# Down-projection of a six-layer attention and feed-forward kernel as nine reduced-precision products, with GpSimd splitting the gated values and the weights

## The reference

```python
def ffn_layer(x, g, bln, W1, b1, W2, b2):
    mu = x.mean(-1, keepdims=True)
    var = ((x - mu) ** 2).mean(-1, keepdims=True)
    xn = (x - mu) / jnp.sqrt(var + 1e-05) * g + bln
    hg = xn @ W1 + b1
    a, gate = jnp.split(hg, 2, -1)
    return a * jax.nn.gelu(gate, approximate=False) @ W2 + b2
for i in range(DEPTH):
    x = attn_layer(shift_tokens(x), Wqkv[i], q_scale[i], k_scale[i], Wo[i]) + x
    x = ffn_layer(shift_tokens(x), ln_g[i], ln_b[i], W1[i], b1[i], W2[i], b2[i]) + x
```

## Time and profile before

| | |
|---|---|
| median of 3 runs | 1655.81 us |
| the profiled execution | 1654.67 us, of which 1652.9 us are the span of the trace |
| TensorE (PE) busy | 95% of the span |
| VectorE (DVE), ScalarE (ACT), GpSimd (POOL) busy | 79%, 77%, 65% |
| one slot of the loop | 30.0 us |

### The profile page before, as it was taken

The page is one execution under the profiler, slowest core; times in us unless marked ns, Lnnn a source line. Parts: engine busy times, 40 slices in busy tenths (PEclk is TensorE's granted clock), DMA queues, the critical chain, the costliest instruction groups (busy, mean ns, idle before and its releaser), DMA issues.

```text
span 1652.9 us, 89828 instructions
## 1 busy us (share of the span) xinstructions
PE 1566.3 (95%) x36944; PEld 1275.7 (77%) x36944; DVE 1305.2 (79%) x1944; ACT 1280.4 (77%) x2012; POOL 1074.3 (65%) x788
## 2 busy tenths in 40 slices
PE   7898699999999999999999999999999999999986
PEld 3575578888888888888888888888888888888865
DVE  5575778788887887888878888888788888887853
ACT  5796557788887888878888788788787887887853
POOL 2203767768767769667678676777776787767631
PEclk9899799999999999999999999999999999999989
DMA  3000224223324232333222342322343323232221
GB/s 128 2 0 1 55 68 113 63 60 75 92 56 113 71 74 65 79 106 82 61 64 69 95 111 57 71 71 65 85 110 75 71 53 91 71 76 63 60 69 34
DMA packets 75728, 116.75 MB, mean 71 GB/s; under 512 B 17294, under 2 KB 27276, under 8 KB 74764
## 3 DMA queue, kind: packets, MB, share of 16 engines
q1 hardware_dynamic: 75660, 115.99, 28.2%
HBM read 19.04 MB, written 1.05 MB: 12 GB/s over the span
## 4 chain that ended last, share of the span: by engine, by line
PE 90%; issue 4%; DVE 3%; ACT 2%; DVEq 0%; POOL 0%; DMA 0%; ACTq 0%; SPq 0%; POOLq 0%
PE ps L646 14%; PE ps L912 10%; PE ps L887 10%; PE ps L838 9%; PE ps L763 9%; PE ps L766 8%; PE ps L767 8%; PE ps L979 4%; PE ps L831 3%; PE ps L928 3%; PE ps L930 2%; PE ps L929 2%; PE ps L635 1%; DVE h L1648 1%; PE ps L919 1%
## 5 line engine op out<-in xcount | busy, mean ns | idle before, releaser
L448 POOL TENSOR_TENSOR arena<-arena 128x1024 f32<-128x1024 f32 x192 | 456.5, 2378 | 74.6 <-DVE arena L1578 60.9
L457 POOL TENSOR_TENSOR arena<-arena,rnorm 128x1024 f32<-128x1024 f32 x192 | 361.7, 1905 | 208.4 <-ACT rnorm L1189 208.3
L646 PE MATMUL ps<-cst,arena 64*128 64x64 f32 x6656 | 290.1, 230 | 27.1 <-issue 6.0
L646 PEld LDWEIGHTS ps<-cst,arena 64*128 64x128 f32 x6656 | 249.1, 140 | 84.8 <-issue 71.3
L1178 ACT ACTIVATE arena<-ps 128x1024 f32<-128x1024 f32 x192 | 196.8, 1025 | 100.7 <-DVE arena L1578 99.6
L1574 DVE TENSOR_TENSOR arena<-ps,rope 128x1024 f32<-128x1024 f32 x192 | 233.8, 1218 | 26.5 <-PE ps L767 26.5
L1578 DVE TENSOR_TENSOR arena<-ps,rope 128x1024 f32<-128x1024 f32 x192 | 233.3, 1215 | 0.0
L766 PE MATMUL ps<-wqkv_lo,x_hi 128*128 128x512 f32 x576 | 228.8, 397 | 0.0
L767 PE MATMUL ps<-wqkv_hi,x_hi 128*128 128x512 f32 x576 | 228.2, 396 | 0.0
L1588 DVE TENSOR_REDUCE norm<-arena 128x16 f32<-128x1024 f32 x192 | 224.5, 1210 | 0.3 <-ACT arena L1178 0.2
L763 PE MATMUL ps<-wqkv_hi,x_lo 128*128 128x512 f32 x576 | 201.4, 431 | 0.6 <-issue 0.6
(11 more groups left out here) (137 smaller groups left out, 2733.7 us busy)
## 6 DMA issues: line engine op xcount, KB each, us to landing
v_sb<-v_nat SPq DMA_DIRECT2D x576, 130.0 KB
v_sb<-v_nat SPq DMA_DIRECT2D x192, 65.0 KB
wqkv_sb<-wqkv SPq DMA_DIRECT2D x6, 1536.0 KB, 6.3
v_sb<-v_sb SPq DMA_DIRECT2D x96, 65.0 KB
wo_sb<-wo SPq DMA_DIRECT2D x6, 512.0 KB, 3.7
w_sb<-w SPq DMA_DIRECT2D x6, 341.0 KB, 4.0
x<-xT SPq DMA_DIRECT2D x1, 1024.0 KB, 4.8
scl<-scales SPq DMA_DIRECT2D x6, 128.0 KB, 6.1
```

The costliest lines, as they stand in the source:

```text
L448: pool.tensor_tensor(t_cos[:, m, j, :], t_cos[:, m, j, :], t_sin[:, j, :], ALU.add)\
L457: pool.tensor_tensor(x, x, rnorm[:, H * j:H * j + H].unsqueeze(2).to_broadcast([P, H, D]), ALU.mult).then_inc(s[done], 1)
L646: mm = pe.transpose(ps[0:width, bank + t, 64 * c:64 * c + 64], src[r], ident[r, r], tile_position=(64 * t, 0))
```

## The change

`f_g` becomes a buffer of its own, and VectorE's product is written in place. GpSimd gets `part_gated` in each slot from 3 to 46: it copies the product, rounded, into `f_ah` and writes the rest into `f_al`. In slots 8L+3 it also gets `split_down`, which does the same with W2 (`w2_hi`, `w2_lo`). TensorE's `down` in the loop becomes `down_parted`, nine matmuls. The units 44 to 47, whose down-projections come behind the loop, keep `down` in float32; units 45 to 47 have a buffer each for the product (`f_last`). Gates now wait until the parts of the unit before are made (`f_parted`) and not for its product. Six buffers are cleared at the start, and two buffers of the first stage move into `arena`.

```diff
+            def part_gated(f):
+                pool.wait_ge(s["f_prod"], CREDIT + 3 * f + 3)
+                pool.wait_ge(s["f_down"], CREDIT + f)
+                pool.sem_inc(s["pool_waited"], 1)
+                pool.tensor_copy(f_ah[:, :, :], f_g[:, :, :]).then_inc(s["f_rounded"], 1)
+                pool.wait_ge(s["f_rounded"], CREDIT + f + 1)
+                pool.tensor_tensor(f_al[:, :, :], f_g[:, :, :], f_ah[:, :, :].bitcast(F32), ALU.subtract)\
+                    .then_inc(s["f_parted"], 1)
+
+            def split_down(layer):
+                pool.wait_ge(s["w_2_loaded"], 32 * layer + 32)
+                pool.wait_ge(s["f_down"], CREDIT + B * layer)
+                pool.sem_inc(s["pool_waited"], 1)
+                for i in (0, 2):
+                    rows, w = (P, slice(0, 2)) if i == 0 else (HT[2][1], slice(2, 3))
+                    pool.tensor_copy(w2_hi[0:rows, w, :], w2_sb[0:rows, w, :]).then_inc(s["w2_high"], 1)
+                    pool.wait_ge(s["w2_high"], CREDIT + 2 * layer + 1 + i // 2)
+                    part = pool.tensor_tensor(w2_lo[0:rows, w, :], w2_sb[0:rows, w, :],
+                                              w2_hi[0:rows, w, :].bitcast(F32), ALU.subtract)
+                part.then_inc(s["w2_ready"], B)
...
                     rotate(g + 1, 0, 0)
                     low(g + 1, 1)
                     rotate(g + 1, 0, 1)
+                    if ff:
+                        part_gated(g - LAG)
+                    if after == 3:
+                        split_down(layer)
                     if after == 7:
                         table(layer, 1)
                         split_weights(layer, 2)
...
+            def down_parted(f):
+
+                pe.wait_ge(s["f_parted"], CREDIT + f + 1)
+                pe.wait_ge(s["w2_ready"], CREDIT + f + 1)
+                out = ps[:, 1, 0:N]
+                for i in range(3):
+                    r = slice(0, HT[i][1])
+                    high = f_ah[r, i, :]
+                    pe.matmul(out, w2_lo[r, i, :], high, start=(i == 0), stop=False)
+                    pe.matmul(out, w2_hi[r, i, :], f_al[r, i, :], start=False, stop=False)
+                    mm = pe.matmul(out, w2_hi[r, i, :], high, start=False, stop=(i == 2))
                 mm.then_inc(s["f_down"], 1)
...
                     if ff:
                         q_read(2 * g + 3)
-                        down(g - LAG)
+                        down_parted(g - LAG)
...
-                act.wait_ge(s["f_prod"], CREDIT + 3 * f)
+                if not last:
+                    act.wait_ge(s["f_parted"], CREDIT + f)
```

More of the change, by code:

```diff
@@ L100, in build @@
         w2_sb = sb("w2_sb", [P, 3, E])
+        w2_hi = sb("w2_hi", [P, 3, E], F32R)
+        w2_lo = sb("w2_lo", [P, 3, E], F32R)
         par = sb("par", [P, L_END])
@@ L156, in build @@
         o_t = take(12288, H // 2, N)
-        f_last = take(8192, 3, N)
+        f_last = {SLOTS - 3 + i: take(768 * i, 3, N) for i in range(3)}
         own = take(6144, 4, N)
@@ L188, in build @@
         a_ks = f_a1[:, 1, :].rearrange("p (k t) -> p k t", k=2)
-        a_vs = f_a2[:, :].rearrange("p (k j h d) -> p k j h d", k=2, j=4, h=2)
+        a_vs = take(10496, CH).rearrange("p (k j h d) -> p k j h d", k=2, j=4, h=2)
         a_p = take(0, 8, N)
@@ L194, in build @@
         a_of = take(10240, 2, P)
-        a_o = f_a3[:, :, :].rearrange("p j (c b h d) -> p j c b h d", c=2, b=2, h=AH)
-        a_o_i = f_a3[:, :, :].rearrange("p j (c i d) -> p j c i d", c=2, d=AD)
+        a_of_all = take(12288, NC, CH)
+        a_o = a_of_all.rearrange("p j (c b h d) -> p j c b h d", c=2, b=2, h=AH)
+        a_o_i = a_of_all.rearrange("p j (c i d) -> p j c i d", c=2, d=AD)
         a_max = sb("a_max", [P, 8])
@@ L235, in build @@
         f_shifted f_mean f_centred f_squared f_var f_log f_rstd f_normed f_scaled
-        f_high f_split w1_high w1_ready
+        f_high f_split w1_high w1_ready f_rounded f_parted w2_high w2_ready
         f_gate_up f_value_up f_gated f_prod f_down f_done
@@ L495, in rest, with slot @@
                 pool.tensor_tensor(f_lo[:, :], f_y, f_hi[:, :].bitcast(F32), ALU.subtract).then_inc(s["f_split"], 1)
-            def slot(g, norm=True, ahead=True, more=True, after=None, layer=None):
+            def part_gated(f):
[17 more added lines that the diff above has]
+                part.then_inc(s["w2_ready"], B)
+            def slot(g, norm=True, ff=True, ahead=True, more=True, after=None, layer=None):
                 f = g - 2
@@ L560, in _ @@
             rotate(0, 1, 1)
-            slot(0, norm=False)
-            slot(1, norm=False)
-            slot(2, after=2, layer=0)
+            slot(0, norm=False, ff=False)
+            slot(1, norm=False, ff=False)
+            slot(2, ff=False, after=2, layer=0)
             with pool.Fori(0, DEPTH - 1) as layer:
                 first = pool.snap(layer * B)
-                with pool.Fori(LAG, 6) as b:
+                slot(pool.snap(first + LAG), after=3, layer=layer)
+                with pool.Fori(LAG + 1, 6) as b:
                     slot(pool.snap(first + b))
@@ L572, in _ @@
                 slot(pool.snap(first + 10), after=2, layer=layer + 1)
-            with pool.Fori(SLOTS - 5, SLOTS - 2) as g:
+            slot(SLOTS - 5, after=3, layer=DEPTH - 1)
+            with pool.Fori(SLOTS - 4, SLOTS - 2) as g:
                 slot(pool.snap(g))
@@ L972, in last_values, with down @@
                 up(ps[:, c, N:2 * N], 0, 1).then_inc(s["f_value_up"], 2)
-            def down(f, bank=1, gated=f_a):
+            def down(f, bank, gated=f_g):
                 pe.wait_ge(s["f_prod"], CREDIT + 3 * f + 3)
-                pe.wait_ge(s["w_2_loaded"], W2_CREDIT + 32 * layer_of(f + B))
+                pe.wait_ge(s["w_2_loaded"], 32 * layer_of(f) + 32)
                 for i in range(3):
@@ L1081, in _ @@
             last_up(g - 1)
-            down(g - 2, 7)
+            down(g - 2, 7, f_last[g - 2])
             last_up(g)
             pe.wait_ge(s["f_done"], CREDIT + g - 1)
-            down(g - 1, 7)
+            down(g - 1, 7, f_last[g - 1])
             pe.wait_ge(s["f_log"], CREDIT + g + 1)
-            down(g, 6, f_last)
+            down(g, 6, f_last[g])
         @block.scalar
@@ L1263, in round_norm, with gate @@
                 act.activation(f_hi[:, :], f_y, ACT.Copy).then_inc(s["f_high"], 1)
-            def gate(f, i, out, count):
+            def gate(f, i, out, count, last=False):
                 size = HT[i][1]
                 act.wait_ge(s["p_h_loaded"], 16 * layer_of(f) + 16)
-                act.wait_ge(s["f_prod"], CREDIT + 3 * f)
+                if not last:
+                    act.wait_ge(s["f_parted"], CREDIT + f)
+                elif f == SLOTS - 3:
+                    act.wait_ge(s["f_down"], CREDIT + f)
+                else:
+                    act.wait_ge(s["f_prod"], CREDIT + 3 * f)
                 act.wait_ge(s["f_gate_up"], CREDIT + 2 * f + count)
@@ L1275, in last_gates @@
                 a, b, c = LAST_BANKS[f]
-                gate(f, 2, ps[:, a, 0:N], 1)
-                gate(f, 0, ps[:, b, 0:N], 2)
-                gate(f, 1, ps[:, b, N:2 * N], 2)
+                gate(f, 2, ps[:, a, 0:N], 1, last=True)
+                gate(f, 0, ps[:, b, 0:N], 2, last=True)
+                gate(f, 1, ps[:, b, N:2 * N], 2, last=True)
             def slot(g, att=True, shifted=True, norm=True, ff=True, ahead=True, more=True, after=None, layer=None):
@@ L1560, in _ @@
             ln_centre(dve, 2, 1)
-            dve.wait_ge(s["zeroed"], 8)
+            dve.wait_ge(s["zeroed"], 14)
             modulate(0)
@@ L1632, in subtract_mean, with product @@
                 dve.tensor_tensor(of[1], of[0], ps[:, bank, 0:N], ALU.subtract).then_inc(s["f_centred"], 1)
-            def product(f, i, value, count, gated=f_a):
+            def product(f, i, value, count, gated=f_g):
                 size = HT[i][1]
-                if gated is f_a:
-                    dve.wait_ge(s["f_down"], CREDIT + f)
                 dve.wait_ge(s["p_h_loaded"], 16 * layer_of(f) + 16)
@@ L1708, in _, with last @@
             slot(g, ahead=False)
-            def last(f, gated=f_a):
+            def last(f):
                 a, b, c = LAST_BANKS[f]
+                gated = f_last[f]
                 product(f, 2, ps[:, a, N:2 * N], 2, gated)
@@ L1731, in _ @@
             last(g - 1)
-            last(g, f_last)
+            last(g)
             add(g - 1, 7)
```

25 lines of the change are left out of this document (14 added, 11 removed).

## The result

The kernel after takes 1646.88 us (median of 5 runs, 1642.22 to 1650.14), the kernel before 1655.81. The ratio is 0.9932, with a 95% interval of 0.9905 to 0.9959. A second set of runs gave 1647.92 us and 0.9939 [0.9916, 0.9962] (both kernels anew). The prediction was 1647.0 us.

The account below looks back on a forecast made before the run. TensorE's own work was taken to bound the loop, with attend idle for VectorE's add; 42 x 0.21 = 8.8 us off 1654.67 gave 1645.9 us for the profiled execution, 1647.0 us for the median, range 1642.5 to 1653.

Parts of the forecast that it names:

- The likeliest case: Start of a slot: attend stops waiting for VectorE's add, then turn_q binds; 0.21 us a slot, 8.8 us in all; 62%.
- Rival 4: Down-projection: each product waits in full for its weight load, nine take 1.7 us; 17.6 us slower, 1673 us; 5%.
- rival 1: Start of a slot: turn_q doesn't bind; each of 44 slots gains 0.25 to 0.33 us, 1641 to 1645 us; 10%.
- rival 3: Start of a slot: attend or turn_q meets another limit at once, almost no gain, 1654 to 1656 us; 8%.
- rival 2: Slots 8L+7 (or 8L+3): GpSimd late, copy_q late, scores waits; 3 to 6 us given back, 1650 to 1653 us; 15%.
- the step from 0.91 to 0.70: Start of a slot: attend's delay behind turn_q's first load falls from 0.91 to 0.70 us, gaining 0.21 us.
- "Everything behind `attend` ... shifts with it": Rest of a slot: all work behind attend hangs on it or turn_q, so the 0.21 us a slot carries through.
- the gap: GpSimd in an ordinary slot: 4.55 us waiting for rnorm, which hides part_gated's 3.3 us, leaving some 1 us idle.
- the gap behind the table: GpSimd, slots 8L+7: 1.42 us idle behind the table takes part of part_gated's delay; L472 begins 1.9 us late.
- the upper price of 1.84: GpSimd's rounding copy of 768 columns at most 1.84 us; in slots 8L+7 that would lose 5 x 0.6 = 3 us.
- The path that I did price: Slots 8L+7: GpSimd's delay through L472 to scale_norm, ScalarE's rounding and copy_q; put at no loss, nothing to spare.

Follow-up runs that it names:

- the six products: Kernel after with six down-projection products in place of nine (w2_lo times f_ah left out): median 1649.08 us, 0.9942 of the kernel before; loop 1278.61 us.
- experiment 6: Trace reading of the kernel after, nothing changed: slots 11 and 27 took 30.03 and 29.96 us; slots 19, 35 and 43, with the same work, 29.78, 29.74 and 29.79.

## Why the prediction was right, and where it was not

**The time and the mechanism.** 1647.0 was forecast, 1646.88 and 1647.92 were measured. The likeliest case is what happened: `turn_q`, held by the copy of v, sets the end of the gain, and the add falls behind it. The products took 0.12 us each (1.25 us from first start to last end, forecast 1.24), and `turn_q` kept its 0.07 us behind the copy. Rival 4 is out by the 0.12, rival 1 by the six products, rival 3 by the slot's own gain and by the view of waits, in which `attend` no longer stands idle for the add. For rival 2 there was no loss in slots 8L+7 (29.74 to 29.82 us), and none in slots 8L+3 that GpSimd caused (slots 11 and 27 are told in experiment 6).

**The size of a slot's gain was too high.** I took 0.21 us, the step from 0.91 to 0.70. The first load of `attend` stands 0.91 behind `turn_q` before and 0.72 after in the mean (0.70 in 23 of 43 slots, 0.74 in 19), which is 0.185. Of that another 0.02 is lost on the way through the slot, half of it in slots 11 and 27. "Everything behind `attend` ... shifts with it" was nearly true: averaged over the slots and counted from the first load of `turn_q`, TensorE's work comes 0.186 earlier at `attend`, 0.179 in the first `up`, 0.168 from the last one and 0.163 at the variance. What is left is 0.165. The two rows from which I took 0.67 and 0.70 were two slots; the spread of their kind was not looked at.

**How often.** I counted 42 slots and left out those at the loop's end. They gained as well: slot 45 went from 30.04 to 29.79. The two that gained nothing were 11 and 27. 43 x 0.165 = 7.1 us against 42 x 0.21 = 8.8. The difference of the medians, 8.9 us, is larger than the loop's 7.1, but its interval (4.1 to 9.5 per thousand, 6.8 to 15.7 us) holds both, and the rest can't be told from the scatter ahead of the loop and behind it. The prediction met the median better than its term deserved.

**GpSimd.** The copy of 768 columns took 0.83 us, not 1.20. The subtraction took 1.82 us (forecast 1.84). In slot 22, against the earlier trace rows:

```profile
851.87 0.84 POOL L509 CAST f_ah<-f_g 128x768 fp32r<-128x768 f32 x1
852.79 1.81 POOL L511 TENSOR_TENSOR f_al<-f_g,f_ah 128x768 fp32r<-128x768 f32 x1
856.53 3.77 POOL L465 TENSOR_TENSOR arena<-arena,rnorm 128x1024 f32<-128x1024 f32 x2 [1.93 <-ACT rnorm L1236]
```

`part_gated` is 2.7 us, not 3.3, and 1.93 us of the gap are left where I expected some 1. The copy of 256 columns takes 0.39 here, so three of them were no good stand-in for one of 768: the start counts three times. By the Trainium skill's page "GPSIMD Engine Reference", section "Elementwise — side-by-side cycle accounting", it would have been an estimated 1.15 us; the measurement decides, 0.83.

**Slots 8L+7: the right result with a step missing.** I wrote that the gap behind the table takes a part of the delay and that the first to feel it is L472. The table itself is waited for in the same slot, which I hadn't followed. In the kernel after, slot 15:

```profile
648.93 1.23 DVE L1626 TENSOR_TENSOR arena<-ps,rope 128x1024 f32<-128x1024 f32 x1 [0.56 <-POOL rope L471]
```

VectorE waits 0.56 us here, and only some 0.3 us more would have been hidden. By estimate from these numbers, had the copy taken the 1.20 us that I priced, these slots would have lost about 0.1 us each; had it taken the upper price of 1.84, 0.7 each, near the 3 us that I gave for it, but by another path.

The path that I did price had 1.0 us to spare in the kernel after, not nothing. In slot 15 the rounding (L1310) still didn't wait for `scale_norm` (L498), which had ended 0.19 us before:

```profile
655.72 0.55 POOL L498 TENSOR_SCALAR f_a<-f_a,par 128x256 f32<-128x256 f32 x1 [0.34 <-POOL f_a L492]
```

```profile
656.46 0.42 ACT L1310 ACTIVATE f_hi<-f_a 128x256 fp32r<-128x256 f32 x1
```

Two errors, the price and the path, covered each other: the right result in these slots was luck.

**Slots 8L+3** held, with `split_down`. What took the gain of two of them is ScalarE's branch.

## What to carry to other kernels

When a wait is removed, look at what stands just behind it before pricing the gain: here it was 0.07 us away, so three products fewer were worth almost nothing, while moving other work into the hole gained 0.20 us a slot, more than the change itself. When work is put ahead of other work on an engine, follow every reader of what it delays, not only the engine's own queue; a short table in between was closer to the bound than the long multiplications behind it. And where runs scatter by several us for what happens ahead of the loop, compare a span of the loop inside the trace: it repeated to 0.1 us.

## What the runs showed of the hardware

- GpSimd's rounding copy grows slowly with size: 0.39 us for 256 columns and 0.83 for 768, 0.84 ns a column, against 2.1 ns for the subtraction (0.74 and 1.82 us).
- ScalarE's branch at the end of the layer loop took from 2.4 to 3.2 us, differing from one turn to the next in the same execution.
- Where the add is long done, `attend` still comes no closer than 0.70 us behind the first load of `turn_q`, whose 16 loads last 0.61 us. In the trace of the kernel after, TensorE's sequencer works through five waits in between, which begin some 0.1 us apart, the last of them 0.63 us behind that first load (0.67 where `attend` comes at 0.74).
